# Attention scores from 32-row products in place of stacked operands, in a two-layer graph kernel

## The reference

```python
h = relu(layernorm(x))
q, k, v = h @ Wq.T, h @ Wk.T, h @ Wv.T + bv          # 12 heads of 32
s = q @ k.T / sqrt(384) + 2 * adj                      # per head, 128 x 128
s = where(any(s != 0, axis=-1), s, -inf); p = nan_to_num(softmax(s))
x = x + concat(p @ v) @ Wo.T + bo
h = relu(layernorm(x))
for l in range(2):                                     # graph layers
    u = triu(adj, 0) * (h @ (h @ Wl[l].T).T) + triu(adj, 1).T * (h @ (h @ Wr[l].T).T)   # both / sqrt(384)
    d = exp(u) * adj
    ctx = (d / (sum(d) + 1e-10)) @ (h @ Wlin.T + blin)
    h = relu(norm(ctx) * a + b)
return x + h
```

## Time and profile before

| | us |
|---|---|
| median of 3 runs | 1607.47 (1607.07 to 1612.33) |
| the profiled execution | 1604.2, of which the span is 1602.4 |
| TensorE busy in the span | 1472.0 (92%) |
| VectorE, ScalarE, GpSimd busy | 1262.0 (79%), 921.5 (58%), 480.6 (30%) |
| transfer engines, mean busy share | about 40% |

### The profile page before, as it was taken

How to read it: one execution, slowest core, us unless ns; L and a number is a source line. 1 busy time by engine, 2 the same in 40 slices (tenths; PEclk the granted TensorE clock), 3 DMA queues, 4 the chain that set the end, 5 groups by cost and what they waited for, 6 DMA issues and landing times.

```text
span 1602.4 us, 38189 instructions
## 1 busy us (share of the span) xinstructions
PE 1472.0 (92%) x12992; PEld 1425.5 (89%) x12992; DVE 1262.0 (79%) x4559; ACT 921.5 (58%) x2091; POOL 480.6 (30%) x926
## 2 busy tenths in 40 slices
PE   4579999999999999999999999999999999999884
PEld 4579999999999999899999999999999999999873
DVE  5468888888888888888788888878888888888853
ACT  4456755556665556566555666655566655556531
POOL 4022323323222332332233333223332323333222
PEclk8689999999999999999999999999999999999986
DMA  8334444443444443444444344334434444443300
GB/s 244 86 74 100 97 97 104 102 100 74 100 96 103 99 107 90 78 102 97 103 98 112 74 93 99 100 97 103 102 78 100 95 98 103 103 110 77 80 1 20
DMA packets 293534, 152.00 MB, mean 95 GB/s; under 512 B 215536, under 2 KB 293104, under 8 KB 293344
## 3 DMA queue, kind: packets, MB, share of 16 engines
q1 hardware_dynamic: 292768, 148.58, 39.8%
q0 software_dynamic: 576, 0.99, 0.3%
HBM read 61.41 MB, written 37.75 MB: 62 GB/s over the span
## 4 chain that ended last, share of the span: by engine, by line
PE 65%; SPq 16%; DMA 10%; DVE 4%; issue 3%; ACT 1%; POOL 1%; DVEq 0%
PE bank L372 56%; SPq L353 14%; DMA pT<-prob_parts 7%; PE bank L441 4%; DMA k<-qk_parts 3%; PE bank L431 2%; PE bank L378 2%; SPq L310 1%; DVE prob L687 1%; PE bank L448 1%; DMA pT<-w 1%; DVE prob_parts L719 0%; DVE h L617 0%; DMA qk_parts<-qk 0%; DVE n L617 0%
## 5 line engine op out<-in xcount | busy, mean ns | idle before, releaser
L372 PE MATMUL bank<-h,weights 128*128 128x256 f32 x3456 | 431.3, 282 | 5.0 <-DVE h L772 4.7
L372 PEld LDWEIGHTS bank<-h,weights 128*128 128x128 f32 x3456 | 413.6, 190 | 6.1 <-issue 6.0
L531 ACT ACTIVATE prob<-prob,rmin 128x128 f32<-128x128 f32 x768 | 245.6, 392 | 19.2 <-DVE rmin L687 8.3
L372 PE MATMUL bank<-weights,h 128*128 128x384 f32 x1152 | 231.6, 345 | 0.0
L372 PE MATMUL bank<-hA,weights 128*128 128x256 f32 x1728 | 222.6, 286 | 2.7 <-DVE weights L593 2.7
L372 PEld LDWEIGHTS bank<-hA,weights 128*128 128x128 f32 x1728 | 215.9, 193 | 3.0 <-issue 3.0
L372 PEld LDWEIGHTS bank<-weights,h 128*128 128x128 f32 x1152 | 194.1, 188 | 0.0
L507 ACT ACTIVATE qk<-bank 128x512 f16<-128x512 f32 x96 | 57.1, 595 | 218.9 <-PE bank L372 218.9
L687 DVE CUSTOM_DVE_ANT_0 prob<-bank,adj_sb 128x128 f32<-128x128 f32 x768 | 176.4, 284 | 0.1
L507 ACT ACTIVATE n<-bank 128x512 fp32r<-128x512 f32 x192 | 113.4, 592 | 104.8 <-PE bank L372 104.7
L617 DVE TENSOR_TENSOR n<-bank,n 128x512 fp32r<-128x512 f32 x192 | 128.6, 684 | 54.4 <-ACT n L507 54.3
(11 more groups left out here) (109 smaller groups left out, 2645.4 us busy)
## 6 DMA issues: line engine op xcount, KB each, us to landing
qk_parts<-qk SPq DMA_DIRECT2D x96, 256.0 KB, 2.5
q<-qk_parts SPq DMA_DIRECT2D x96, 192.0 KB, 4.5
k<-qk_parts SPq DMA_DIRECT2D x96, 192.0 KB, 5.4
x_sb<-x SPq DMA_DIRECT2D x32, 384.0 KB, 4.3
out<-x SPq DMA_DIRECT2D x32, 384.0 KB, 2.9
pT<-prob_parts SPq DMA_TRANSPOSE x384, 2.5
adj_sb<-adj SPq DMA_DIRECT2D x32, 128.0 KB, 2.2
x<-w SPq DMA_DIRECT2D x3, 576.0 KB, 5.1
```

Source lines behind the costliest of these rows:

```text
L372: mm = pe.matmul(out, lhsT, rhs, start=(n == 0), stop=(n == len(pairs) - 1))
L531: e = act.activation(prob[:, h, :], prob[:, h, :], ACT.Exp, bias=rmin[:, j, h:h + 1], scale=-1.0)
```

## The change

The stacks go. `qk` becomes two buffers, by the parity of the group, and the scores are taken straight from it: head h = c * 4 + a lies in block c on the partitions 32a to 32a + 31. A score of a head is three products of 32 rows, summed in PSUM; the four a's use the four row groups of the array, each with its own bank, and the three c's lie side by side in the bank. All 36 products of a graph are one block at step `S03` or `S13` (the other three S entries of TensorE's list only wait for their bank). `prob` is ordered by a, so VectorE, ScalarE and the split work by a: eight S and x steps of three heads; `ph`, `pl` and the transposing transfers take six heads (two a's), eight transfers a group. `xn1` gets its own tile. BANK and ORDER are new for all engines.

```diff
-        qk = sb("qk", [P, 2, 2 * C, T], F16)
-        xn1 = qk[:, :, :, :].rearrange("p s c t -> p (s c t)").bitcast(F32).rearrange("p (g h) -> p g h", g=2 * G)[:, 0:G, :]
-        qk_dram = nc.dram_tensor("qk_parts", [2, P, 2, 2 * C, T], F16).ap()
-        q3 = sb("q3", [3 * D, NH, T], F16)
-        k3 = sb("k3", [3 * D, NH, T], F16)
+        qk = sb("qk", [P, 2, 2, 2 * C, T], F16)
+        xn1 = sb("xn1", [P, G, H])
...
-                    for a in range(HC):
-                        mm = pe.matmul(bank(step)[:, a * P:(a + 1) * P], q3[:, a * C + c, j * P:(j + 1) * P], k3[:, a * C + c, j * P:(j + 1) * P], start=True, stop=True)
-                    mm.then_inc(full(step), 1)
+                    j, last = int(step[1]), int(step[2])
+                    if last == HC - 1:
+                        for k in range(3):
+                            wait_drained(pe, f"QK{k}", g)
+                        js = slice(j * P, (j + 1) * P)
+                        for c in range(C):
+                            for n, (u, v) in enumerate(PARTS):
+                                for a in range(HC):
+                                    rs = slice(a * D, (a + 1) * D)
+                                    mm = pe.matmul(bank(f"S{j}{a}")[:, c * P:(c + 1) * P], qk[rs, g % 2, u, c, js], qk[rs, g % 2, v, C + c, js],
+                                                   start=(n == 0), stop=(n == len(PARTS) - 1))
+                                    if (c, n) == (C - 1, len(PARTS) - 1):
+                                        mm.then_inc(full(f"S{j}{a}"), 1)
...
-                    for k in range(3):
-                        ge(act, s_qs[k], 16 * g)
...
-                    wait_drained(act, f"S{j}{c}", g)
-                    for h in range(c * HC, (c + 1) * HC):
+                    wait_drained(act, f"S{j}{a}", g)
+                    for h in range(a, NH, HC):
...
-                    hs = slice(c * HC, (c + 1) * HC)
+                    hs = slice(2 * b * C, 2 * (b + 1) * C)
...
 ORDER = {
     "SP": [
-        ("ptl11", 0), ("pth10", 0), ("ptl10", 0), ("ld_adj", 1), ("out", -2), ("qs1", 1), ("qs0", 1), ("qs2", 1), ("ld_x", 2),
-        ("q3", 1), ("k3", 1), ("pth02", 1), ("ptl02", 1), ("pth00", 1), ("ptl00", 1), ("pth01", 1), ("ptl01", 1), ("pth12", 1),
-        ("pth11", 1), ("ptl12", 1)],
+        ("ld_x", 2), ("ld_adj", 2), ("pth01", 1), ("pth00", 1), ("ptl00", 1), ("ptl01", 1), ("pth10", 1), ("ptl10", 1),
+        ("pth11", 1), ("ptl11", 1), ("out", -1)],
     "PE": [
...
+        ("WO1", 0), ("N10", -1), ("N11", -1), ("N12", -1), ("HL10", -1), ("T2b", 0), ("T2a", 0), ("U1", -1), ("S02", 1),
+        ("S00", 1), ("S01", 1), ("S03", 1), ("HL11", -1), ("AT", 0), ("N01", 0), ("S10", 1), ("C11", -1), ("C10", -1),
+        ("N02", 0), ("T1a", 2), ("N00", 0), ("S12", 1), ("S11", 1), ("HL00", 0), ("S13", 1), ("HL01", 0), ("T1b", 2), ("U0", 0),
+        ("PV0", 1), ("QK0", 2), ("QK1", 2), ("C00", 0), ("C01", 0), ("QK2", 2), ("OT0", 1), ("V0", 2), ("PV1", 1), ("WO0", 1),
+        ("OT1", 1), ("HTb", 0), ("HTa", 0), ("V1", 2)],
...
     "DVE": [
...
+        ("QK2", 1), ("HTb.h", -1), ("HTa.h", -1), ("HTb.l", -1), ("HTa.l", -1), ("WO1", 0), ("ln2_st", 0), ("ln2_ag", 0),
+        ("N10", -1), ("ln1_st", 2), ("N11", -1), ("ln1_ag", 2), ("V0", 1), ("N12", -1), ("HL10", -1), ("V1", 1), ("T2b", 0),
+        ("T2a", 0), ("U1.m", -1), ("U1.w", -1), ("S01", 1), ("U1.d", -1), ("U1.dh", -1), ("HL11", -1), ("U1.dl", -1),
+        ("S03", 1), ("S02", 1), ("S00", 1), ("C11", -1), ("C10", -1), ("gst11", -1), ("gst10", -1), ("N01", 0), ("gag1", -1),
+        ("pl01", 1), ("pl00", 1), ("r00", 1), ("N02", 0), ("N00", 0), ("T1a", 2), ("S11", 1), ("S13", 1), ("S10", 1),
+        ("S12", 1), ("HL00", 0), ("T1b", 2), ("U0.m", 0), ("y0", -1), ("U0.w", 0), ("pl10", 1), ("U0.d", 0), ("y1", -1),
+        ("U0.dh", 0), ("PV0.r", 1), ("U0.dl", 0), ("HL01", 0), ("PV0.n", 1), ("pl11", 1), ("PV0.o", 1), ("C00", 0), ("C01", 0),
+        ("gst00", 0), ("gst01", 0), ("gag0", 0), ("QK1", 2), ("QK0", 2), ("OT0", 1), ("r01", 1), ("PV1.r", 1), ("PV1.n", 1),
+        ("PV1.o", 1), ("WO0", 1), ("OT1", 1)],
```

More of the change, by code:

```diff
@@ L71 @@
 BANK = {
[L72 to L79, removed]
+    0: ["N12", "S00", "HL00", "QK2"],
+    1: ["HL11", "C11", "T1a", "U0", "V1"],
+    2: ["WO1", "T2a", "S10", "QK0", "WO0"],
+    3: ["N10", "S03", "S12", "QK1", "HTa"],
+    4: ["HL10", "S02", "S11", "PV0", "PV1", "HTb"],
+    5: ["N11", "S01", "N02", "HL01", "OT0", "OT1"],
+    6: ["T2b", "AT", "C10", "N00", "T1b", "C00"],
+    7: ["U1", "N01", "S13", "C01", "V0"],
 }
@@ L221, in build @@
         s_xbo = [sem(f"x_plus_bo{j}") for j in range(G)]
[L222 to L226, removed]
+        s_exp = [[sem(f"exps{j}{a}") for a in range(HC)] for j in range(G)]
+        s_part = [[sem(f"prob_{n}{b}") for b in range(2)] for n in ("hi", "lo")]
+        s_turned = [[sem(f"prob_turned_{n}{b}") for b in range(2)] for n in ("hi", "lo")]
         s_stats = {k: sem(f"stats_{k}") for k in ("ln1", "ln2")}
@@ L252, in build @@
         SPLIT_AFTER = {
-            "ACT": {"": (0,), "xn1_1": (1,), "T1b": (2, 3), "QK1": (4, 5), "QK0": (6,), "QK2": (7,), "V1": (8,), "V0": (9,)},
-            "DVE": {"ln1_ag": (0,), "T1b": (1, 2), "QK1": (3, 4), "QK0": (5,), "QK2": (6, 7), "V1": (8,), "V0": (9,)}}
+            "ACT": {"": (0,), "xn1_1": (1,), "T1b": (2, 3), "QK1": (4, 5), "QK0": (6,), "QK2": (7,), "V0": (8,), "V1": (9,)},
+            "DVE": {"ln1_ag": (0,), "T1b": (1, 2), "QK1": (3, 4), "QK0": (5,), "QK2": (6, 7), "V0": (8,), "V1": (9,)}}
         def staged(m):
@@ L294, in build @@
         PARTS = [(HI, HI), (HI, LO), (LO, HI)]
-        STACKED = 16 * 3
         block = ctx.enter_context(nc.Block())
@@ L305, in load_weights @@
                     sp.dma_start(staged(m), w_d[m].rearrange("(c p) o -> p c o", p=P)).then_inc(s_wload[STAGE_OF[m]], 16)
[L307 to L310, removed]
             def run(step, g):
@@ L319, in run @@
                     for j in range(G):
-                        for c in range(C):
-                            wait_drained(sp, f"S{j}{c}", g - 2)
+                        for a in range(HC):
+                            wait_drained(sp, f"S{j}{a}", g - 2)
                     wait_filled(sp, "AT", g - 2)
@@ L324, in run @@
                     sp.dma_start(adj_sb[:, p, :, :], adj_d[g * G:(g + 1) * G, :, :].rearrange("g p h -> p g h")).then_inc(s_adjin[p], 16)
[L325 to L341, removed]
                 elif step[:2] == "pt":
-                    part, j, c = "hl".index(step[2]), int(step[3]), int(step[4])
-                    hs = slice(c * HC, (c + 1) * HC)
+                    part, j, b = "hl".index(step[2]), int(step[3]), int(step[4])
+                    hs = slice(2 * b * C, 2 * (b + 1) * C)
                     if g == 0:
                         sp.wait_ge(s_wlo, NW)
-                    sp.wait_ge(s_part[part][c], G * g + j + 1)
+                    sp.wait_ge(s_part[part][b], G * g + j + 1)
                     if j == 0:
@@ L426, in run @@
                 elif step[0] == "S":
-                    j, c = int(step[1]), int(step[2])
-                    pe.wait_ge(s_q3, STACKED * (g + 1))
-                    pe.wait_ge(s_k3, STACKED * (g + 1))
-                    for a in range(HC):
-                        mm = pe.matmul(bank(step)[:, a * P:(a + 1) * P], q3[:, a * C + c, j * P:(j + 1) * P], k3[:, a * C + c, j * P:(j + 1) * P], start=True, stop=True)
-                    mm.then_inc(full(step), 1)
+                    j, last = int(step[1]), int(step[2])
[5 more added lines that the diff above has]
+                            for n, (u, v) in enumerate(PARTS):
+                                for a in range(HC):
+                                    rs = slice(a * D, (a + 1) * D)
[3 more added lines that the diff above has]
+                                        mm.then_inc(full(f"S{j}{a}"), 1)
                 elif step[:2] == "PV":
@@ L436, in run @@
                     for part in (HI, LO):
-                        for c in range(C):
-                            pe.wait_ge(s_turned[part][c], 16 * (G * g + j + 1))
+                        for b in range(2):
+                            pe.wait_ge(s_turned[part][b], 16 * (G * g + j + 1))
                     for h in range(NH):
                         for n, (a, b) in enumerate(PARTS):
-                            mm = pe.matmul(bank(step)[:, h * DA:(h + 1) * DA], pT[:, a, h, :], v2[:, b, j, h, :],
+                            mm = pe.matmul(bank(step)[:, h * DA:(h + 1) * DA], pT[:, a, h % HC * C + h // HC, :], v2[:, b, j, h, :],
                                            start=(h == 0 and n == 0), stop=(n == 2), skip_group_check=True)
@@ L522, in run @@
                     k = int(step[2])
-                    hi(step, g, qk[:, HI, 2 * k:2 * k + 2, :], 2 * T, "p (c t) -> p c t", c=2)
+                    hi(step, g, qk[:, p, HI, 2 * k:2 * k + 2, :], 2 * T, "p (c t) -> p c t", c=2)
                 elif step[0] == "V":
```

(16 more changed lines are left out.)

38 lines of the change are left out of this document (20 added, 18 removed), and 25 rows, old and new, of the table ORDER.

## The result

The changed kernel takes 1525.82 us (median of 4 runs, 1525.23 to 1527.04) against 1607.27 (1604.98 to 1612.33) for the kernel before in the same session: the ratio is 0.949, 95% interval 0.947 to 0.951. I had forecast 1596 and a range of 1568 to 1648.

A forecast was written before the change was run, and what follows sets the result against it. TensorE's own instructions, few waits and the two ends were taken to decide. The period falls from 46.88 to 46.7 us, thirty give -5 us, ends -6: 1593 us profiled, 1596 median; range 1568 to 1648.

The forecast's parts named there:

- I take 1.15 us: Time on TensorE of one block of 36 score products of 32 rows; range 0.9 to 2.15 us, two blocks a period.
- the bound from below: Score block no shorter than PV's 36 weight-load-and-product pairs: 0.92 us, 25.6 ns each.
- Some 0.8 are small waits and slow-clock pieces: Part of TensorE's 44.1 us a period left after the removals; the small waits were left as they are.
- the change of product kind: One change of product kind fewer on TensorE, taken as 0.1 us less a period.
- Place (a): PV1 waiting for transpose ptl11, by SyncE's queue or VectorE's work: 0 to 1.6 us a period, 0.4 taken.
- (b): VectorE's parts for WO0 ready at 10.8 against 11.4 us, HTb's rows at 13.3 against 13.25; no wait if VectorE is never late.
- (c): x, loaded after WO1, must give N12 for U1 by 9.9 us, due at the median; 0 taken, 1.3 us worst.
- Rival 2: VectorE and its queues become the bound at the three tight places: period 48.0 us, time 1635 us; chance 0.16.
- The ends, -6 us: Start gains 10 us or so without waits for stacks; the end loses some 4 us.
- The gap of 4 us: At the end, PV0 and PV1 of the last groups have no QK between them, opening some 4 us.
- Nine transfers at no cost in the middle: Removing nine stack transfers a group (three out, six back) was given no price in the middle.
- Rival 3: Score blocks at the issue floor (0.95 us) and no PV1 wait: period 45.9 us, time 1571 us; chance 0.14.

The follow-up runs named there:

- six and eight pieces: Changed kernel with six, or eight, transposes of graph 1 behind PV0 in place of four: 1548.08 us and 1649.14 us.
- a outermost: Changed kernel with the loop over the four row groups outermost in a score block, nine products in a row on one row group: 1581.38 us.

## Why the prediction was wrong

The mechanism was the one forecast, TensorE's list plus its waits, less the old waits; four terms of the sum were mis-sized, all to one side. The forecast period was 46.7 us, the measured one 44.89. Of the 70 us between 1596 and 1525.8, thirty periods are 54 and the ends 12; the rest is that the profiled execution now is not 3 us below the median.

- **The score block, "I take 1.15 us".** It is 0.61, or 0.70 with the 0.09 on entering it. Twice 0.54 are 1.08 us a period, the largest error. The step that failed is the bound from below: "the block cannot be shorter" than PV's 36 pairs at 25.6 ns. PV's pairs take all 128 rows; on four row groups four pairs take 56 ns, 14 each. So 25.6 ns is no floor of the issue of a weight load and a product. What holds PV's pairs at 25.6 no run here isolates. No value that I could choose inside the bounds was right.
- **"Some 0.8 are small waits and slow-clock pieces", left as they are.** About 0.3 of them went. Without the score steps the period was 45.65 us and is 43.68. The waits that I had taken off are 1.5 of these 2.0, and the change of product kind 0.1; some 0.3 are left over. The slow-clock pieces are at most 0.17 of it. The rest is spread over U0 with T1a, the N steps and C00 and C01 of the table, less the 0.27 by which other steps grew. I had no reason to keep them but caution.
- **Place (a), "PV1 waits 0 to 1.6 us; I take 0.4".** It waits 0.0. The issue of a six-head transpose was at the lower end, 1.22 us, and the removed 1.31 us came in full. The runs with six and eight pieces show that the queue's arithmetic is of the right kind and reads about 1 us too high.
- **Places (b) and (c).** No waits, as taken. But the margins were not nil: from the records the medians are 0.89 us from OT0's parts to WO0, 0.57 from the normed rows to HTb and 0.62 from N12's parts to U1, where I had 0.6, 0 and 0. (The terms of (b) as printed add up to 10.7 and 9.0 us, not 10.8 and 9.2; nothing hangs on it.) Rival 2 was given 0.16 on that walk; VectorE with 0.94 us more work costs 0.30 us a period, so it would have needed 0.6 us more work than there is.
- **The ends, -6 us.** They gave 18.3. The scores of group 0 begin as forecast right behind V, at 34.62 us in place of 39.67, and of group 1 at 73.4 in place of 84.3. In front of those of group 1 stands another wait, 5.2 us for the second norm of group 0:

```profile
34.62 0.68 PE L407 MATMUL bank<-qk 32*128 32x128 f16 x36
...
71.93 1.51 PE L348 MATMUL bank<-ident,o_sb 128*128 128x128 f32 x6 [5.21 <-ACT o_sb L522]
73.37 1.15 PE L407 MATMUL bank<-qk 32*128 32x128 f16 x36
```

  The gap of 4 us that I forecast for the last groups is there (3.82 us before C00, then 1.31 before PV1), but waits of the old tail went too, and from the start of U0 of group 30 to the end it takes 91 us now and took 94. So most of the 18 was won at the start. The run with stacks in the new order shows that 7 to 8 of them are the stacks'. How the others divide between the list and the clock (0.91 in place of 0.77 in the second stretch) no run here separates.
- **Nine transfers at no cost in the middle** was right, and so was xn1's tile at nothing, though T1a's wait, which I put down to the stacks, stayed without them (4.9 us) and is absent with the new order, with stacks or without.
- **The range.** Its low end, 1568, rested on the false floor of the block and on small waits that stay. Rival 3 (0.14) was the nearest case, with both too large: with 0.61 for 0.95 and 0.3 us of small waits less, 45.9 becomes 44.9.

What the parts of the change are worth, by the runs: the new order and banks with the fused transposes, but the old operands, give 79 us of the some 82. Of these 23 hang on having four transposes behind PV0 and not six. The rest is the order and the banks, which no run separates. The new operands give 4 us: they win at the start, where the DRAM round trip is gone, and the 32-row products pay a little back in the middle (44.89 us a period against 44.80). With a outermost they would have cost 56 us.

## What to carry to other kernels

When an engine is at 92 to 95%, add up its own list from start to start of each step without waits: what lies above it is what a new order can win. Here that sum tells the result within 1% once the block's measured 0.61 us stands in it: 44.1 + 2 x 0.61 = 45.3 us against 44.89. A row bounds an unknown operation only if the same thing limits both; ask what sets the pace in the row before calling it a floor. When transfers stand between two steps of the bound engine, count the queue's instructions first, and their bytes second: one issue of twelve heads took 1.4 to 1.8 us here, three of four heads take 3.9.

## What the runs showed of the hardware

Products of 32 rows by 128 columns on four row groups, each with its own PSUM bank, start 3 ns apart and take 56 ns for four; on one row group they follow at 56 ns (changed kernel, a outermost). A transposing transfer costs its issuer 1.22 us for four or six heads (128 columns of fp16 each) and 1.43 or 1.83 for twelve, and lands after 2.5, 2.8 and 3.8 to 4.2 us (medians). In front of a block of 32-row products a step takes 0.08 to 0.09 us more than in front of one of 96-row products. Behind the block, the next step begins 144 ns after the last product's start, where products of one row group follow at 56.
